# ScalarE's order in slot 0 of a chunk: copy, two exponentials, copy in place of two exponentials, two copies

## What is computed

```
xn     = group_norm(x)                       # 32 groups of 8 channels, x is (4, 256, 64*64)
f, g   = Wq @ xn, Wk @ xn                    # 64 x 4096 each
h      = Wv @ xn                             # 256 x 4096
scores = f^T g                               # 4096 x 4096 for each image
beta   = softmax(scores, over the rows n)
out    = x + (gamma * (h @ beta) + xn)
```

## Time and profile before

| | value |
|---|---|
| median of 3 runs | 1918.55 us |
| the profiled execution's own time | 1918.76 us |
| its span, first to last instruction | 1917.0 us |
| TensorE matmul busy | 1886.6 us, 98% |
| VectorE busy | 1631.2 us, 85% |
| ScalarE busy | 1578.0 us, 82% |
| GpSimd busy | 1307.8 us, 68% |
| mean granted TensorE clock | 0.997 |

### The profile page before, as it was taken

One profiled execution on the slowest core, in us unless ns is written; L12 is line 12 of the kernel. 1 busy time (PEld: TensorE's weight loads), 2 busy tenths in 40 slices (PEclk: granted clock), 3 DMA queues, 4 the chain that ended last, 5 costly groups with the idle time before them and its releaser, 6 DMA issues. The chain is left out here.

```text
span 1917.0 us, 44195 instructions
## 1 busy us (share of the span) xinstructions
PE 1886.6 (98%) x17369; PEld 1555.9 (81%) x17369; DVE 1631.2 (85%) x2238; ACT 1578.0 (82%) x1677; POOL 1307.8 (68%) x757
## 2 busy tenths in 40 slices
PE   7899999999999999999999999999999999999999
PEld 4678888877888888887888888888788888888888
DVE  7889998987879999888877999998787788888885
ACT  4788888988768888987877888899787788888885
POOL 4367668876556776886664766788665577767777
PEclk9999999999999999999999999999999999999999
DMA  4022212212102221211211221122121111111111
GB/s 144 4 67 57 67 31 59 66 30 52 44 21 73 75 56 23 76 53 23 70 37 40 53 70 53 37 65 53 29 65 31 22 32 34 24 33 31 33 32 37
DMA packets 200111, 91.19 MB, mean 48 GB/s; under 512 B 150240, under 2 KB 191712, under 8 KB 199904
## 3 DMA queue, kind: packets, MB, share of 16 engines
q1 hardware_dynamic: 199904, 88.36, 17.8%
HBM read 46.60 MB, written 16.78 MB: 33 GB/s over the span
## 5 line engine op out<-in xcount | busy, mean ns | idle before, releaser
L390 POOL TENSOR_TENSOR PL<-SC,PH 128x1024 f16<-128x1024 f32 x511 | 1092.2, 2143 | 549.9 <-ACT SC L643 544.4
L505 PE MATMUL O<-V,PH 128*128 128x257 f16 x4096 | 1119.1, 273 | 0.1
L507 PE MATMUL O<-V,PL 128*128 128x257 f16 x4096 | 1118.8, 273 | 0.0
L506 PE MATMUL O<-V,PH 128*128 128x256 f16 x4096 | 1117.3, 273 | 0.0
L636 ACT ACTIVATE SC<-S 128x1024 f32<-128x1024 f32 x512 | 504.1, 1013 | 136.8 <-issue 122.7
L884 DVE TENSOR_TENSOR SC<-SC,MB 128x1024 f32<-128x1024 f32 x511 | 613.6, 1211 | 0.1
L642 ACT ACTIVATE PH<-SC 128x1024 f16<-128x1024 f32 x511 | 539.4, 1056 | 84.0 <-PE O L507 62.7
L643 ACT ACTIVATE SC<-SC 128x1024 f32<-128x1024 f32 x511 | 532.8, 1043 | 0.0
L841 DVE TENSOR_TENSOR XM<-S,XM 128x1024 f32<-128x1024 f32 x384 | 468.6, 1220 | 74.4 <-PE S L493 64.7
L506 PEld LDWEIGHTS O<-V,PH 128*128 128x128 f16 x4096 | 401.1, 98 | 51.0
L507 PEld LDWEIGHTS O<-V,PL 128*128 128x128 f16 x4096 | 401.1, 98 | 50.1
(11 more groups left out here) (117 smaller groups left out, 1029.4 us busy)
## 6 DMA issues: line engine op xcount, KB each, us to landing
xin<-x SPq DMA_DIRECT2D x24, 1024.0 KB, 5.6
xres<-x SPq DMA_DIRECT2D x64, 256.0 KB, 3.0
ATT<-OT SPq DMA_DIRECT2D x1008, 16.0 KB, 1.8
out<-RES SPq DMA_DIRECT2D x63, 256.0 KB, 2.2
SC<-x SPq DMA_DIRECT2D x8, 512.0 KB, 7.1
F<-GG SPq DMA_DIRECT2D x64, 64.0 KB, 2.0
GG<-GG SPq DMA_DIRECT2D x32, 128.0 KB, 2.4
SC<-wvT SPq DMA_DIRECT2D x1, 256.0 KB, 7.1
```

The lines of the kernel that those rows point to most:

```text
L390: pool.tensor_tensor(PL[:, s % RING, :], sc(s), PH[:, s % RING, :], ALU.subtract).then_inc(pl_ready, 1)
L505: mm(o[:, 0:C + 1], PH[:, n % RING, cols], vh, start=t == 0, stop=False)
L506: mm(o[:, 0:C], PH[:, n % RING, cols], vl, start=False, stop=False)
L507: w = mm(o[:, 0:C + 1], PL[:, n % RING, cols], vh, start=False, stop=t == T - 1)
```

## The change

For slot 0 of every chunk from k = 1 to k = 61 ScalarE's `store(q)` is moved from behind `exps(n + 3)` to ahead of it. `store(q + 1)` stays behind. All other slots, chunk 0 and the two last chunks keep their order. No instruction, wait or semaphore is added or taken away.

```diff
--- before.py
+++ after.py
@@ -699,11 +699,14 @@
             for n in range(K * G):
                 k, g = divmod(n, G)
                 b, j = divmod(k, CPB)
+                q = SCORES_AT.get(n)
+                if g == 0 and k > 0 and q is not None:
+                    store(q)
                 if k > 0 and n + EXP_LEAD < K * G:
                     exps(n + EXP_LEAD)
-                q = SCORES_AT.get(n)
                 if q is not None:
-                    store(q)
+                    if g > 0 or k == 0:
+                        store(q)
                     store(q + 1)
                 if k == 0:
                     for s in FIRST_EXP[g]:
```

## The result

The changed kernel takes 1910.15 us (median of 6 runs, 1908.85 to 1911.46) against 1918.67 us for the kernel before (6 runs): 0.9956 of the time, 95% interval 0.9943 to 0.9969. The forecast was 1911.0, in a range from 1909.0 to 1914.8. The profiled execution took 1910.60 us, its span is 1908.9 us in place of 1917.0.

A forecast was written before the change was run, and what follows sets the result against it. TensorE was busy 98% of the span, so only its 9.6 us of stalls could be gained. 5.0 + 2.7 = 7.7 us off 1918.76 gave 1911.1 us, forecast as 1911.0, range 1909.0 to 1914.8.

The forecast's parts named there:

- all that there is to gain: TensorE's stalls in front of `scores` from 109 us on: together 9.6 us, 0.5% of 1917.
- all three kinds: Stalls before `scores`: for VectorE's maximum 5.3 us, without a named releaser about 2.9 us, for V's remainder 1.4 us.
- The places of the three moved instructions: After slot 0's `scores` start: even copy at +1.50, line 836 at +2.73, odd copy at about +4.35 us.
- Cause (a): Normalising chunks, slots 4 and 6: line 836 1.65 us earlier, so stalls for VectorE's maximum go; taken as 5.0 us.
- Cause (b): Slot 6 of chunk 14: `regroup` 1.07 us earlier, so the last `move_f` no longer stalls `scores`; 2.7 us.
- The sum: 5.0 us in normalising chunks plus 2.7 us in chunk 14: 7.7 us off the profiled execution's 1918.76 us.
- the fourth wait without a releaser: One of four waits before `scores` with no named releaser, 3.3 us together; the other three are slot 6 of chunk 14.
- Cause (c): Chunk 0: V's copy waits for TensorE and not for the odd copy; no gain of the 1.4 us expected.
- The delay: `exps(n + 3)` ends at about +4.4 instead of +3.27 us; GpSimd's line 390 behind it has over 4 us cover, cost nothing.
- The marks: Expected trace signs: waits for line 841 from 27 to a few, without releaser from 3.3 to under 0.7 us.
- The rule on table sets: Skill's advice to batch ScalarE activations by set; alone it would cost an estimated 325 us; the forecast added nothing.

The follow-up runs named there:

- e9: Changed kernel, plus SyncE sending chunk 14's last `move_f` before the 16 DMAs and VectorE making V's remainder before the maxima reduction in chunk 0; 1908.80 us, 0.9952.
- e3: Against the kernel before, the even copy moved in all chunks but 1, 6, 8 to 11 and 14; 1913.90 us, 0.9978.
- e2: Against the kernel before, the even copy moved in chunk 14 of each image alone; 1916.24 us, 0.9992.
- e4: Kernel before with ScalarE's order kept; SyncE sends the last `move_f` in chunk 14 ahead of the 16 DMAs; 1915.53 us, 0.9986.
- e7: Against the changed kernel, slot 0 copies both the even and odd halves ahead of the two exponentials; 1926.05 us, 1.0044.
- e1: Against the kernel before, the even copy moved only in chunk 1 and chunks 6 and 8 to 11 of each image; 1912.68 us, 0.9968.

## Why the prediction was right

- *What bounds it, and all that there is to gain (9.6 us).* Right. e9, which takes away all three kinds, gains 9.66 us from chunk 1 to the last scores. Reading the stalls from the weight loads' waits, less 0.11 us each, gave 5.3, 2.9 and 1.4. That the two agree to 0.1 us is in part luck: 0.2 of the 9.6 us lie in front of slot 0 of chunk 1 and so outside that stretch, and 0.3 of the 9.66 us are the late starts of 0.01 us, which the waits do not show.
- *The places of the three moved instructions.* Right to 0.03 us in chunk 9. The even scores' 1.50 us, read in the one slot where ScalarE had waited for nothing else, held: line 836 is at +2.73 in 60 of the 61 chunks, and at +3.29 in chunk 1, where VectorE is free no earlier. One reading was off without effect: ScalarE waits 1.06 us for the even scores there and not 0.24, since in the changed kernel it reaches slot 0 of that chunk earlier than it did before.
- *Cause (a), 5.0 us.* The size was right (5.0). The step that named the cause was incomplete: it took VectorE's idle 2.01 us in that chunk for the origin of that chunk's stall. e3 showed that the lateness builds up over chunks, 0.37 us in each, and that a moved copy in chunk 7 frees chunks 8 and 9. The sum did not suffer, as the change moves the copy in all of them.
- *Cause (b), 2.7 us.* The chain was right (e2, e4), and `regroup` was 1.07 us earlier. The term was 2.3: in image 0 the 16 DMAs took 0.45 us longer to send. The forecast had allowed up to 0.3 for each; 0.43 is more than that.
- *The sum, 7.7 us against 7.79.* Closer than its terms. (b) gave 0.4 us less than its term, and 0.55 us had no term: the short late starts (0.3) and the fourth wait without a releaser (0.26), which the sum of all stalls had in its 2.9 us but (a), (b) and (c) did not. The two nearly cancel, which is luck.
- *Cause (c), no gain for V.* Right, 1.8 us of waits in place of 1.7. e9 shows what was wrong there: the order on VectorE.
- *The delay, costed at nothing.* Right as to the time, wrong as to its cover. The 8.57 us of GpSimd in the earlier trace rows begin with the remainder for slot 2, not for slot 3. The one for slot 3 is the second of the four and ended at 802.12 + 2 x 2.14 = 806.4 = +8.8, so its cover before +11.0 was 2.2 us and not over 4. After the change, in a narrower window that shows the first two of the four:

```profile
797.11 4.26 POOL L390 TENSOR_TENSOR PL<-SC,PH 128x1024 f16<-128x1024 f32 x2
```

  Slot 3's remainder, the second, ends at 801.37 = +7.8, and TensorE has no wait for line 390.
- *The marks.* Waits for 841 "to a few" (one), without releaser "under 0.7" (0.5), V's as before, no wait of line 487 for line 636 from 109 us on: all seen. One mark was wrong: line 836's idle time was to be near 0 to 0.4 us and is 0.88 in chunk 9, for VectorE too comes to slot 0 earlier than before.
- *The rule on table sets.* Copy, Exp, Exp, Copy start 0.92, 0.94 and 0.95 us apart above (795.06, 795.98, 796.92, 797.87), and the changed kernel too has a single table load: the alternation costs nothing. The Trainium skill, "ScalarE: Activation LUTs", section "Table sets: the hidden batching unit", says that copy is in every set; this trace agrees.

## What to carry to other kernels

When an engine is at 98%, list its few late starts with place and releaser and follow each back until an idle engine or a queue is found: here three tenths of the stalls were a queue of small DMAs four steps behind the moved copy. In a hand-written order put first what another engine waits for, and behind it work that has slack; but an instruction that itself waits for that other engine belongs behind the work with slack, as e7 shows, 15.6 us slower than the change from chunk 1 to the last scores. And compare the rounds of coupled engines over several chunks, not one chunk alone: a lateness of 0.37 us a chunk shows first as idle time without harm, and as a stall only some chunks on.

## What the runs showed that had not been expected

- The time to send the same 16 DMAs of 16 KB varied between 10.25 and 11.86 us within and between runs, and in chunk 14 this set whether and how long TensorE stood still (none up to 10.82 us, 0.43 us at 11.29, 0.92 us at 11.78).
- Chunks without a stall can carry half of a gain: e3 moved no copy in a chunk where TensorE had waited for line 841 or for `move_f` and gained 4.0 us.
- The parts do not add up: e1, e2 and e3 gain 5.5, 2.1 and 4.0 us, 11.6 together, and the whole 7.8, since e1 and e3 both take away the stalls of chunks 6, 8 and 9 and a part of those of chunks 10.
- The first 109 us vary by up to 2.6 us between executions (107.3 to 109.9), while the 1746 us from chunk 1 to the last scores agree to 0.13 us in the two executions profiled of the changed kernel.
